# Attention and shared-expert kernel on one core: GpSimd's share of the routing tiles, the order at the pass boundary and at the start, and a matmul on half of the array's rows

## The chip, the cores and the metric

One core of a Trainium2 chip runs the whole program. The metric is the device time of one execution in microseconds. Engines: TensorE (PE; its weight loads are PEld), VectorE (DVE), ScalarE (ACT), GpSimd (POOL) and SyncE (SP), which issues most of the DMAs.

## The reference

64 batches of 128 tokens of 512 numbers, all float32:

```python
x = x + tanh(g_xattn) * attention(layernorm(x), ctx, ctx)    # 32 heads of 16, 8 key/value heads, 128 keys a batch
x = x + tanh(g_ffn) * moe(layernorm(x))

# moe: h is layernorm(x), 8192 tokens
probs = softmax(h @ Wr); topw, topi = top_k(probs, 4); topw /= topw.sum(-1)
shared = silu(h @ Wsg) * (h @ Wsu) @ Wsd * sigmoid(h @ Wse)  # inner width 1408
# the first 64 (token, rank) pairs of each of 32 experts, in token order, go through that expert (inner width 352):
ye = (silu(xe @ Wg) * (xe @ Wu)) @ Wd
out = shared + sum over a token's kept experts of topw * ye
```

## The kernel before

**Attention.** `iterations` runs the batches one after the other on every engine, with the work of several batches interleaved in four steps c = 0 to 3 of a fixed order. PE transposes keys (L645) and queries (L653), computes scores twice: once with queries as rows, for the maxima (L746, into `p_max`), which DVE reduces (L589), and once with keys as rows (L694, into `p_exp`), which ACT exponentiates (L467); then values times probabilities (L669, four tiles of 32 columns), transposes back (L679), transposes the normalised rows (L704) and multiplies with the router's weights (L720). In L694, a step's 128 rows of `kt` hold the stacked parts of two key heads, 64 rows each; the other half of the columns is zero in each, so that one full-height matmul serves one head. ACT's `k_evac` (L444, L445) copies the transposed keys; L669 at c = 0 also waits for it.

At the start DVE clears the padding (`vals`, `qs`, `kt`, `ks`), then takes the statistics of the first batch; POOL computes 1/sqrt (`inverse_root`, L335 and L339), DVE normalises (L537), POOL stacks the high and low parts of keys (`k_stacks`, L347 to L350) and queries (`q_stacks`, L366, L370). POOL's body for batch 0 does them in the order `inverse_root(0)`, `k_stacks(0)`, `q_stacks(0)`, `inverse_root(1)`.

**Shared expert.** The 8192 tokens are 16 tiles of 512. The inner width of 1408 is 11 blocks of 128; the weights of all don't fit on the chip, so there are two passes over the tiles: `Tile(0, i)` with five blocks, `Tile(1, i)` with six. The gate and up products of a block are one 2 x 2 product by Winograd's scheme with seven products (`product`, L1498 to L1500; each in three parts, as every operand is split in a high and a low part). A step f of a tile does: products 1 and 2, then products 6 and 7 of the step before (`last_two`), then 3, 4, 5. DVE adds up (L1427 c11, L1398 c12, L1434 c22), ACT applies SiLU (L1151), DVE multiplies (L1401, L1404), ACT takes the high part `hh` (L1158, `high`), DVE the low part `hl` (L1411, `low`):

```python
                def low(T, f):
                    s = T.step + f
                    dve.wait_ge(hh_done, s + 1)
                    if f == 0:
                        wait(dve, acc_mm, TB * T.n)
                    nc.vector.tensor_tensor(hl[:, f, :], act_g(T), hh[:, f, :].bitcast(F32), ALU.subtract).then_inc(hl_done, 1)
```

`silu` on ACT waits for the low part of the step before, and ACT's copy `term` (L1176) of the next step stands behind it; product 3 waits for `term`, product 7 for c22. At the end of a tile PE does the down products (`down`, L1521 to L1523), four blocks of 128 tokens, and DVE adds each to the output rows (`add_acc`, L1418). Between these adds DVE and ACT prepare the next tile's tokens: loads on SP, four sums (L1249), high parts on ACT (L1144), seven low parts on DVE (L1256).

**Routing.** Tiles 1 to 3 of the first pass carry, in DVE's `work` of each step and one at a tile's end, the search for each expert's first tokens: `key_step` alternates MAX8 (L1307) and MATCH_REPLACE8 (L1309) over 2048 elements; in tile 3 `merge_step` follows. The first step of tile 1 also has `route_weights`. POOL in the meantime splits weights: `down_low` (L1024), `wide_sums` (L1034 to L1040) and the low part of the wide weights for block 5 in one instruction of 1792 elements (L1076). It then waits for the routing.

**Experts.** From tile 4 on, a pair of experts rides on two tiles: `Pair(p, xt, gu, ht, dn)` gives the steps in which PE transposes the gathered rows (L1558), does gate and up (L1567), transposes (L1573) and does down (L1580). In the second of the two tiles `adds` is set: POOL gathers output rows (L1101), DVE adds (`add_rows`, L1344) in steps 1 and 3, POOL scatters them (L1106), first for one expert, then for the other; SP loads the tile's own rows (`load_rows`, L943) when both are through.

**Pass boundary.** The last tile of the first pass, `Tile(0, 15)`, prepares the tokens of tile 0 for `Tile(1, 0)`, as any tile does for its next. In tile 15 POOL runs `wide_sums(1)` to `(5)`, ACT and DVE split the first of these weights (`wide_high(1)`, `wide_low(1)`, L1271), before the first add; the others come in the steps of `Tile(1, 0)`.

The functions that the change touches:

## Time and profile before

| | |
|---|---|
| median of 3 runs | 2221.2 us (2220.02 to 2221.82) |
| the profiled execution | 2219.52 us, its span 2217.7 us |
| granted clock of PE, mean | 0.998 |
| busy: PE, PEld, DVE, ACT, POOL | 98%, 82%, 68%, 53%, 29% |
| the chain that ended last | PE 91%, DVE 5%, issue 1%, DMA 1%, ACT 1% |
| attention | up to about 665 us |
| first pass, second pass | about 665 to 1373 us, 1373 to 2215 us |

A row of the timeline has the start in us, the duration in us (of all that it merges), engine, line, operation, output and inputs, shapes and how many; in brackets the idle time of the engine before it and what ended it. A matmul's record lasts longer than its slot, as matmuls are pipelined: the distance between starts is what it costs. Idle time of an engine that isn't the bottleneck costs nothing.

### The profile page before, as it was taken

The numbers are of one execution on the slowest core, as the hardware profiler recorded it, in microseconds if no ns is written. First come the engines' busy times: TensorE is split into PE (matmuls) and PEld (weight loads), VectorE is DVE, ScalarE is ACT, GpSimd is POOL, SyncE is SP. The second block draws the span as 40 slices with busy tenths as digits, with TensorE's granted clock in tenths as the row PEclk, the third lists the DMA queues.
The fourth block names the chain that finished last, engine by engine and source line by source line (L and its number), as shares of the span: only waits on it lengthen the run. The fifth ranks groups of instructions, "written<-read, shape, count | busy, mean of one in ns | idle before, by whom it ended". The sixth has DMA issues, their size and how long they took to land.

```text
span 2217.7 us, 53973 instructions
## 1 busy us (share of the span) xinstructions
PE 2175.7 (98%) x17121; PEld 1820.9 (82%) x17121; DVE 1517.9 (68%) x3135; ACT 1182.9 (53%) x2365; POOL 652.9 (29%) x1492
## 2 busy tenths in 40 slices
PE   7999999999999999999999999999999999999999
PEld 5777777777768888988888888788898989888888
DVE  6999999999997885655655556655554555555554
ACT  6899999999985333334334434433333333333332
POOL 5778777877773000000100104100010000001100
PEclk9999999999999999999999999999999999999999
DMA  3555555555553324443443444424333423344431
GB/s 87 153 147 152 145 152 146 152 145 152 147 154 124 77 68 157 136 146 116 142 151 102 149 150 148 143 65 147 105 107 100 137 87 127 135 149 153 151 96 62
DMA packets 320316, 286.27 MB, mean 129 GB/s; under 512 B 124753, under 2 KB 238417, under 8 KB 320210
## 3 DMA queue, kind: packets, MB, share of 16 engines
q1 hardware_dynamic: 315858, 272.24, 40.6%
q0 software_dynamic: 4352, 12.65, 2.2%
q8 instruction: 62, 1.02, 0.2%
q14 instruction: 44, 0.36, 0.1%
HBM read 195.43 MB, written 88.34 MB: 128 GB/s over the span
## 4 chain that ended last, share of the span: by engine, by line
PE 91%; DVE 5%; issue 1%; DMA 1%; ACT 1%; POOL 0%; DVEq 0%; ACTq 0%; POOLq 0%; SPq 0%
PE p_a L1498 8%; PE p_a L1499 7%; PE p_a L1500 7%; PE acc L1521 7%; PE acc L1523 6%; PE acc L1522 6%; PE p_pv L669 6%; PE p_max L746 6%; PE p_exp L694 5%; PE p_tq L653 5%; PE p_c L1498 3%; PE p_c L1500 3%; PE p_c L1499 3%; PE p_ot L679 2%; PE p_x L1580 2%; PE p_y L1567 2%
## 5 line engine op out<-in xcount | busy, mean ns | idle before, releaser
L1498 PE MATMUL p_a<-x_h,ws_h 128*128 128x256 f32 x1280 | 374.6, 293 | 11.9 <-DVE chosen L1434 7.4
L1499 PE MATMUL p_a<-x_l,ws_h 128*128 128x256 f32 x1280 | 358.3, 280 | 0.0
L1500 PE MATMUL p_a<-x_h,ws_l 128*128 128x256 f32 x1280 | 357.9, 280 | 0.0
L589 DVE TENSOR_REDUCE negmax<-p_max 128x8 f32<-128x1024 f32 x256 | 313.7, 1225 | 40.9 <-PE p_max L746 38.1
L1151 ACT ACTIVATE chosen<-chosen 128x256 f32<-128x256 f32 x342 | 142.3, 417 | 365.0 <-DVE chosen L1398 208.2
L1521 PE MATMUL acc<-wd_h,hh 128*128 128x512 f32 x704 | 280.1, 398 | 5.1 <-DVE rows L1418 3.7
L1522 PE MATMUL acc<-wd_l,hh 128*128 128x512 f32 x704 | 278.0, 395 | 0.0
L1523 PE MATMUL acc<-wd_h,hl 128*128 128x512 f32 x704 | 278.0, 395 | 0.0
L467 ACT ACTIVATE probs<-p_exp 128x1024 f32<-128x1024 f32 x256 | 261.5, 1021 | 24.0 <-PE p_exp L694 19.6
L1498 PEld LDWEIGHTS p_a<-x_h,ws_h 128*128 128x128 f32 x1280 | 241.1, 188 | 31.9 <-issue 14.4
L1499 PEld LDWEIGHTS p_a<-x_l,ws_h 128*128 128x128 f32 x1280 | 241.9, 189 | 0.6
L1427 DVE TENSOR_TENSOR chosen<-p_b,term 128x256 f32<-128x256 f32 x171 | 72.5, 424 | 246.6 <-PE p_b L1500 152.6
L1500 PEld LDWEIGHTS p_a<-x_h,ws_l 128*128 128x128 f32 x1280 | 241.3, 188 | 0.0
L1084 POOL COPY cur_u<-slot_idx 128x1 uint32 (+1 forms) x16 | 3.7, 230 | 711.1 <-DVE cur_f L1383 594.3
L1144 ACT ACTIVATE x_h<-x_raw 128x512 fp32r<-128x512 f32 x221 | 121.9, 619 | 153.7 <-DVE x_raw L1249 147.7
L1434 DVE TENSOR_TENSOR chosen<-p_a,term 128x256 f32<-128x256 f32 x171 | 72.5, 424 | 175.1 <-PE p_a L1500 174.5
L746 PE MATMUL p_max<-kt,qt 128*128 128x256 f32 x1024 | 184.5, 302 | 1.8 <-DVE negmax L589 1.8
L1498 PE MATMUL p_c<-x_h,ws_h 128*128 128x256 f32 x640 | 180.8, 282 | 0.0
L1499 PE MATMUL p_c<-x_l,ws_h 128*128 128x256 f32 x640 | 179.2, 280 | 0.0
L1176 ACT ACTIVATE term<-p_a 128x256 f32<-128x256 f32 x176 | 66.1, 375 | 212.1 <-PE p_a L1500 207.4
L1500 PE MATMUL p_c<-x_h,ws_l 128*128 128x256 f32 x640 | 179.2, 280 | 0.0
L1521 PEld LDWEIGHTS acc<-wd_h,hh 128*128 128x128 f32 x704 | 132.0, 187 | 46.2 <-issue 9.3
(209 smaller groups left out, 5351.2 us busy)
## 6 DMA issues: line engine op xcount, KB each, us to landing
rows<-out_dram SPq DMA_DIRECT2D x32, 1024.0 KB, 7.2
out_dram<-rows SPq DMA_DIRECT2D x128, 256.0 KB, 2.1
x_raw<-xn_cols SPq DMA_DIRECT2D x124, 256.0 KB, 2.9
ew<-in_L_ffn_Wg_dram SPq DMA_DIRECT2D x32, 704.0 KB, 6.0
ew<-in_L_ffn_Wu_dram SPq DMA_DIRECT2D x32, 704.0 KB, 7.7
xs<-in_x_dram SPq DMA_DIRECT2D x64, 256.0 KB, 2.7
xres<-in_x_dram SPq DMA_DIRECT2D x64, 256.0 KB, 2.8
out_dram<-x SPq DMA_DIRECT2D x64, 256.0 KB, 2.6
```

Source lines behind the costliest of these rows:

```text
L467: nc.scalar.activation(probs[c][:, :], p_exp[:, :, :].rearrange("p a b -> p (a b)"), ACT.Exp, scale=float(D) ** -0.5).then_inc(exp_done, 1)
L589: nc.vector.tensor_reduce(negmax[c // 2][:, :].rearrange("p (g c i) -> p c i g", g=2, c=2)[:, c % 2, :, :], p_max[:, :, :].rearrange("p a ...
L669: last = mm(p_pv[32 * q:32 * q + 32, :], vals[b.par][:, g, :], probs[2 * s + q // 2][:, 512 * (q % 2):512 * (q % 2) + 512], start=True, st ...
L746: last = mm(p_max[:, i // 2, 256 * (i % 2):256 * (i % 2) + 256], qt[B.par][:, c, 128 * i:128 * i + 128], kt[B.par][:, c, :], start=True, s ...
L1144: nc.scalar.activation(x_h[:, k, :, :], block(k), ACT.Copy).then_inc(xhi_done, 1)
L1151: nc.scalar.activation(act_g(T)[:, cols], gate(T)[:, cols], ACT.Silu).then_inc(silu2_done if half else silu1_done, 1)
L1498: mm(bank, w_h[:, a, k, :], x_h[:, b, k, :], start=start and k == 0, stop=False, skip_group_check=not start)
L1499: mm(bank, w_h[:, a, k, :], x_l[:, b, k, :], start=False, stop=False, skip_group_check=not start)
L1500: last = mm(bank, w_l[:, a, k, :], x_h[:, b, k, :], start=False, stop=(k == 1), skip_group_check=not start)
L1521: mm(bank, hh[:, f, t], wd_h[:, d, :], start=(f == 0), stop=False)
L1522: mm(bank, hh[:, f, t], wd_l[:, d, :], start=False, stop=False)
L1523: last = mm(bank, hl[:, f, t], wd_h[:, d, :], start=False, stop=(f == T.nf - 1))
```

## The change

- `qs` and `kt` are cleared by POOL and not by DVE, right after its first constants, counted by a semaphore of their own (`padded`), on which ACT and PE wait; POOL's first batch does `k_stacks(0)` before `inverse_root(0)`.
- L694 for even c: each of the two matmuls reads only its own 64 rows of `kt` and `qt`.
- In tiles 1, 2 and 3 of the first pass the low parts of all steps but the last are taken by POOL (`routed_low`), ahead of its wait for the routing; DVE's `low` does the last one alone and waits for the others.
- POOL's low part of the wide weights is seven instructions, each waited for; `down_low` waits for its own end too.
- The second pass handles the tokens in the order 15, 0, 1, ... 14 (`Tile.data`): `Tile(1, 0)` uses the tokens that `Tile(0, 15)` has on the chip, and neither tile 15 nor the last one prepares tokens (`Tile.loads`); counts of prepared tiles go by `Tile.xn`.
- `wide_low(1)` stands behind the first add of tile 15.
- Pair 0 does its transposes, gate and up, and second transposes one step later, `Pair(p, 1, 2, 3, 4)`; in tile 15 the first `add_rows` comes in step 2 and not 1.

```diff
@@ -202,7 +202,7 @@
             consts, tanh_done = sem("consts"), sem("tanh_done")
-            pads, id0 = sem("pads"), sem("id0")
+            pads, padded, id0 = sem("pads"), sem("padded"), sem("id0")
@@ -325,7 +325,10 @@
                 pool.wait_ge(id0, 3)
-                pool.wait_ge(pads, 8)
+                for i in range(2):
+                    nc.gpsimd.memset(qs[i][:, :, :, :, 0:16], 0.0).then_inc(padded, 1)
+                    nc.gpsimd.memset(kt[i][:, :, :].bitcast(F32), 0.0).then_inc(padded, 1)
+                pool.wait_ge(pads, 5)
@@ -402,8 +405,8 @@
                     if isinstance(B.n, int) and B.n == 0:
+                        k_stacks(B)
                         inverse_root(B, stat1, mv1, ve1, rs1, qraw_done, rs1_done)
-                        k_stacks(B)
@@ -436,7 +439,7 @@
                 nc.scalar.activation(tanh_f[:, :], gf[:, :], ACT.Tanh).then_inc(tanh_done, 1)
-                act.wait_ge(pads, 8)
+                act.wait_ge(padded, 4)
@@ -503,10 +506,6 @@
                     nc.vector.memset(vals[i][:, :, 16:17], 1.0).then_inc(pads, 1)
-                for i in range(2):
-                    nc.vector.memset(qs[i][:, :, :, :, 0:16], 0.0).then_inc(pads, 1)
-                nc.vector.memset(kt[0][:, :, :].bitcast(F32), 0.0)
-                nc.vector.memset(kt[1][:, :, :].bitcast(F32), 0.0).then_inc(pads, 1)
@@ -634,7 +633,8 @@
                 pe.wait_ge(consts, 1)
-                pe.wait_ge(pads, 8)
+                pe.wait_ge(pads, 5)
+                pe.wait_ge(padded, 4)
@@ -691,7 +691,8 @@
                             for g2 in range(2):
-                                last = mm(p_exp[:, g2, :], kt[b.par][:, c, 128 * g2:128 * g2 + 128], qt[b.par][:, c, :],
+                                own = slice(64 * g2, 64 * g2 + 64) if c % 2 == 0 else slice(0, 128)
+                                last = mm(p_exp[:, g2, :], kt[b.par][own, c, 128 * g2:128 * g2 + 128], qt[b.par][own, c, :],
@@ -872,6 +873,23 @@
+                @property
+                def data(self):
+                    if self.part == 0:
+                        return self.i
+                    return NT - 1 if self.at(1, 0) else self.i - 1
+                @property
+                def xn(self):
+                    return self.n - self.part
+                @property
+                def loads(self):
+                    return not (self.last or self.at(0, NT - 1))
@@ -885,7 +903,9 @@
                         t.flip = j * t.nf % 2
-                        pair = Pair(p, 0, 1, 2, 4) if j == 0 and p is not None else None
+                        pair = None
+                        if j == 0 and p is not None:
+                            pair = Pair(p, 1, 2, 3, 4) if isinstance(p, int) and p == 0 else Pair(p, 0, 1, 2, 4)
@@ -973,14 +993,14 @@
                         sp.wait_ge(eo_out, 32 * (adds + 1))
-                    load_rows(T.i)
+                    load_rows(T.data)
...
                         next_down(3)
-                    if not T.last:
-                        i = 0 if T.at(0, NT - 1) else T.i + 1
+                    if T.loads:
+                        i = T.i + 1 - T.part
@@ -999,7 +1019,7 @@
                         sp.wait_ge(add_done, TB * T.n + j + 1)
-                        sp.dma_start(out_rows[bass.ts(TB * T.i + j, 128), :], rows[:, j, :]).then_inc(rows_out, 16)
+                        sp.dma_start(out_rows[bass.ts(TB * T.data + j, 128), :], rows[:, j, :]).then_inc(rows_out, 16)
@@ -1023,6 +1043,7 @@
                                             ALU.subtract).then_inc(dlo_done, 1)
+                    pool.wait_ge(dlo_done, s + 1)
@@ -1073,9 +1094,20 @@
                 pool.wait_ge(wshi_done, 1)
-                nc.gpsimd.tensor_tensor(w5_l[:, :, :, :], raw_slot(0), w5_h[:, :, :, :].bitcast(F32), ALU.subtract).then_inc(wslo_done, 1)
-                pool.wait_ge(route_out, 32)
-                pool.wait_ge(slots_done, 1)
+                for k in range(NW - 1):
+                    chain.inc(nc.gpsimd.tensor_tensor(w5_l[:, k, :, :], raw_slot(0)[:, k, :, :], w5_h[:, k, :, :].bitcast(F32), ALU.subtract))
+                    chain.wait(pool)
+                nc.gpsimd.tensor_tensor(w5_l[:, NW - 1, :, :], raw_slot(0)[:, NW - 1, :, :], w5_h[:, NW - 1, :, :].bitcast(F32),
+                                        ALU.subtract).then_inc(wslo_done, 1)
+                def routed_low(T, f):
+                    s = T.step + f
+                    pool.wait_ge(hh_done, s + 1)
+                    pool.wait_ge(hl_done, s)
+                    if f == 0:
+                        pool.wait_ge(acc_mm, TB * T.n)
+                    nc.gpsimd.tensor_tensor(hl[:, f, :], act_g(T), hh[:, f, :].bitcast(F32), ALU.subtract).then_inc(hl_done, 1)
@@ -1109,6 +1141,11 @@
+                for i in range(1, 4):
+                    for f in range(NF[0] - 1):
+                        routed_low(Tile(0, i), f)
+                pool.wait_ge(route_out, 32)
+                pool.wait_ge(slots_done, 1)
@@ -1223,8 +1260,8 @@
                         wide_high(1)
-                    if not T.last:
-                        split_x(T.n + 1, low_block)
+                    if T.loads:
+                        split_x(T.xn + 1, low_block)
@@ -1345,7 +1382,7 @@
                     wait(dve, add_done, TB * T.n)
-                    nc.vector.tensor_copy(cur_g[:, :], gate_s[:, bass.ts(T.i, TB)]).then_inc(wcur_set, 1)
+                    nc.vector.tensor_copy(cur_g[:, :], gate_s[:, bass.ts(T.data, TB)]).then_inc(wcur_set, 1)
@@ -1383,7 +1420,7 @@
                         scale_rows(e)
-                    if adds is not None and f == 1:
+                    if adds is not None and f == (2 if T.at(0, NT - 1) else 1):
@@ -1405,6 +1442,11 @@
                     s = T.step + f
+                    routed = T.part == 0 and isinstance(T.i, int) and 0 < T.i < 4
+                    if routed and f < T.nf - 1:
+                        return
+                    if routed:
+                        dve.wait_ge(hl_done, s)
@@ -1442,23 +1484,23 @@
                     low(T, T.nf - 1)
-                    if T.at(0, NT - 1):
-                        wide_low(1)
...
                     add_acc(T, 0)
-                    n = T.n + 1
-                    if not T.last:
-                        dve.wait_ge(xb_in, 32 * (T.n + 1))
-                        dve.wait_ge(xa_in, 32 * (T.n + 1))
+                    n = T.xn + 1
+                    if T.at(0, NT - 1):
+                        wide_low(1)
+                    if T.loads:
+                        dve.wait_ge(xb_in, 32 * n)
+                        dve.wait_ge(xa_in, 32 * n)
...
                         route_end()
-                    if not T.last:
+                    if T.loads:
@@ -1493,7 +1535,7 @@
                     if f == 0:
-                        pe.wait_ge(xlo_done, NX * T.n + ORDER.index(b) + 1)
+                        pe.wait_ge(xlo_done, NX * T.xn + ORDER.index(b) + 1)
```

## Rows read from the trace of the kernel before

**Rows 1.** page of the profile, busy time, share and instructions of each engine

```profile
PE 2175.7 (98%) x17121; PEld 1820.9 (82%) x17121; DVE 1517.9 (68%) x3135; ACT 1182.9 (53%) x2365; POOL 652.9 (29%) x1492
```

**Rows 2.** waits of TensorE over the whole span: us in total, times, longest

```profile
PE p_pv L645 <- POOL ks L350: 8.7, 1, 8.7
PE p_a L1498 <- DVE chosen L1434: 7.4, 6, 3.0
PE acc L1521 <- DVE rows L1418: 3.7, 4, 2.9
PE p_x L1558 <- DMA xe<-xn_rows,cur_u: 1.9, 1, 1.9
```

**Rows 3.** windows: 100 to 400 us, busy time (instructions) of each engine, clock, DMA share, GB/s

```profile
100.00:400.00 300.00, 299.95 (x3164) 223.12 (x3163) 284.84 (x628) 273.00 (x462) 236.97 (x611) 1.00 0.56 149
```

**Rows 4.** timeline of the start, GpSimd: start, us, engine, line, operation

```profile
0.74 0.20 POOL L319 MEMSET ident<- 128x128 f32 x1 [0.29 <-POOLq L1643]
6.23 0.24 POOL L335 TENSOR_SCALAR small<-small 128x1 f32<-128x1 f32 x1 [4.42 <-DVE small L528]
8.56 1.51 POOL L366 TENSOR_SCALAR qs<-qraw 128x256 fp32r<-128x256 f32 x4
```

**Rows 5.** timeline, TensorE around its one matmul of 32 rows

```profile
838.44 0.40 PE L1523 MATMUL acc<-wd_h,hl 128*128 128x512 f32 x1
838.76 0.21 PE L1596 MATMUL p_y<-ident,ew 32*64 32x32 f32 x1
838.91 0.50 PE L1521 MATMUL acc<-wd_h,hh 128*128 128x512 f32 x1
```

**Rows 6.** timeline, TensorE around L694 at c = 0 and c = 2

```profile
202.14 0.73 PE L694 MATMUL p_exp<-qt,kt 128*128 128x512 f32 x2
202.80 0.16 PEld L669 LDWEIGHTS p_pv<-probs,vals 128*32 128x32 f32 x8 [0.36 <-ACT kt L445]
207.06 0.62 PE L694 MATMUL p_exp<-qt,kt 128*128 128x512 f32 x2
207.62 1.06 PE L669 MATMUL p_pv<-probs,vals 128*32 128x512 f32 x8
```

**Rows 7.** timeline, the first L1427 of tiles 2 to 6 on VectorE

```profile
763.19 0.41 DVE L1427 TENSOR_TENSOR chosen<-p_b,term 128x256 f32<-128x256 f32 x1
805.58 0.41 DVE L1427 TENSOR_TENSOR chosen<-p_b,term 128x256 f32<-128x256 f32 x1
847.61 0.42 DVE L1427 TENSOR_TENSOR chosen<-p_b,term 128x256 f32<-128x256 f32 x1
898.91 0.42 DVE L1427 TENSOR_TENSOR chosen<-p_b,term 128x256 f32<-128x256 f32 x1 [0.55 <-PE p_b L1500]
937.77 0.42 DVE L1427 TENSOR_TENSOR chosen<-p_b,term 128x256 f32<-128x256 f32 x1 [0.35 <-PE p_b L1500]
```

**Rows 8.** timeline, step 1 of tile 2 on ScalarE and VectorE

```profile
769.06 0.62 ACT L1158 ACTIVATE hh<-chosen 128x512 fp32r<-128x512 f32 x1
771.13 0.68 DVE L1411 TENSOR_TENSOR hl<-chosen,hh 128x512 fp32r<-128x512 f32 x1
772.68 0.42 DVE L1427 TENSOR_TENSOR chosen<-p_b,term 128x256 f32<-128x256 f32 x1 [0.87 <-ACT term L1176]
```

**Rows 9.** timeline, GpSimd and VectorE in step 1 of tile 1

```profile
720.58 1.29 POOL L1024 TENSOR_TENSOR wd_l<-wd_raw,wd_h 128x512 fp32r<-128x512 f32 x1 [20.23 <-ACT wd_h L1130]
721.83 4.05 POOL L1076 TENSOR_TENSOR w_l<-w_raw,w5h_l 128x1792 fp32r<-128x1792 f32 x1
722.38 3.78 DVE L1404 TENSOR_TENSOR chosen<-chosen 128x256 f32<-128x256 f32 x1 [0.15 <-ACT chosen L1151]
```

**Rows 10.** windows: 853.1 to 856.5 us

```profile
853.10:856.50 3.40, 3.40 (x18) 3.40 (x18) 0.85 (x2) 0.80 (x2) 0.00 (x0) 0.50 0.78 294
```

**Rows 11.** timeline, VectorE at the end of tile 15

```profile
1370.04 5.76 DVE L1256 TENSOR_TENSOR x_l<-x_raw,x_h 128x512 fp32r<-128x512 f32 x6
```

**Rows 12.** timeline, GpSimd in tile 15

```profile
1343.53 0.95 POOL L1101 DMA_INDIRECT chosen<-out_dram,cur_u  x1 [2.57 <-DMA out_dram<-chosen,cur_u]
```

## The prediction

> **What bounds the kernel now.** I read the page's engine shares first, then the waits of TensorE, then stretches of the timeline. TensorE (PE) is busy 98% of the span; the next engine, VectorE (DVE), has 68% [rows 1]. So a microsecond counts only where PE loses it: in a wait, in a matmul slot longer than need be, or at half clock. The waits add up to about 40 us, and the large ones have addresses: the first batch's keys (8.7), the second product of the step before, released by DVE's L1434 (7.4), the output adds L1418 (3.7) and the gathered rows of the first expert pair (1.9) [rows 2]. In the attention part nothing shows as a wait (PE 299.95 of 300), but DVE is busy 284.84 of the same 300 us [rows 3]: what PE gives up there, DVE can follow by 5% at most.
>
> **The start.** GpSimd (POOL) sits idle until DVE's first statistics, works `inverse_root` and the key stack from 6.23 and the query stack from 8.56, 2.33 us later [rows 4]. The change puts the clears of `qs` and `kt` on POOL (2 of 512 and 2 of 1024 elements each) and the key stack ahead of `inverse_root`. The nearest POOL row is a clear of 128 elements in 0.20 us [rows 4]; taken to scale beyond a fixed tenth, the four cost about 2.9 us, from 1.9 to 4.9, while the inputs land. Then the same 2.33 of work, now with `inverse_root` last, ends at 7.2. DVE's normalisation (about 0.7) starts no earlier than now, but the query stack follows it at 7.95 and no longer stands behind the key stack until 8.56: **-0.6 us**. The clears could cost nearly nothing (then the same, since the statistics wait for x) or twice as much (+2.9 us on this chain): from -0.6 to +2.3.
>
> **The second score product, L694.** For even c each of its two matmuls now uses 64 rows of the array, one the upper half and one the lower, into two banks. If they run side by side, a slot of 2 x 0.23 becomes one of 0.23. What it costs is a change of the array's shape. The trace has one such change: L1596 (32 rows) starts 0.32 after a 512-column matmul whose slot is 0.23, so 0.09 for draining, and the next full matmul lasts 0.50 where its like last 0.40, because its weights could not be loaded ahead: 0.10 [rows 5]. Today the pair at c = 2 starts at 207.06 and the column-tiled L669 follows at 207.62: 0.56, in which the second change (into L669's shape) is already paid [rows 6]. New: 0.09 + 0.10 + 0.23 + 0.09 = 0.51, a gain of 0.05. At c = 0 the gain would be larger (its slot is 0.66 today), but there L669 is released by the key evacuation on ACT (L445) [rows 6], which hangs on the exponentials and not on this slot; it is clipped to almost nothing. 63 batches x 0.05 is **-3 us**. Bounds: with no price for the change of shape the gain is the whole 0.23 at c = 2, -14.5 us; with no overlap the slots become 0.74 for 0.56 and 0.66, +16 us.
> The Trainium skill (TensorEngine Tiling (Array Packing), Key Properties) says that tiles load weights and multiply independently, and that changing the tiling mode drains the engine. The 0.09 of [rows 5] agrees with the second; no trace here shows two row tiles at once, so the first is what the term rests on beyond the rows. Column tiles do overlap: L669's eight records take 1.06 in all [rows 6].
>
> **Tiles 1 to 3 of the first pass.** They carry the routing steps on DVE. A plain tile takes 937.77 - 898.91 = 38.9 us, tile 2 42.4 and tile 3 42.0 [rows 7]. In their steps DVE runs a key search of 2.3 us, then c22, then the low part L1411 (0.68), and only then may ACT's SiLU, its copy `term` and DVE's next L1427 go: a ring of 5.8 us where PE needs 5.0. In step 1 of tile 2 the high part is there at 769.68, but L1411 comes at 771.13 and ends at 771.81; L1427 follows at 772.68, waiting for ACT's `term` [rows 8]. On POOL the low part starts at once and takes what L1024 takes for the same shape, 1.29 [rows 9]: done at 771.05, 0.76 earlier. The ring falls to about 5.0 and PE bounds it. First steps keep their loss of 0.8 (search before c22, no low part involved), and the merge steps of tile 3 are longer than the searches by half a microsecond. So **-2.4** of tile 2's 3.5 and **-1.4** of tile 3's 3.1.
> Tile 1 is worse: DVE's L1404 lasts 3.78 there and not 0.42, for POOL's L1076 (4.05, one instruction of 1792 elements) holds the memory port [rows 9]. Cut in seven, the product gets in after at most one piece (0.6), and c22 comes 2.8 us earlier. But the same queue now holds the tile's low part: seven pieces at 0.81 (the spacing of POOL's chained 256-element operations) end near 727.8, the low part of step 0 near 729.1, SiLU and `term` at 730.0, against 729.84 to 730.2 now. The wait moves from L1434 to `term`. What is left is the faster ring of the last two steps: **-1.0**. The 2.7 us at 720.6 (route weights and search before c22) stay.
> Does POOL's low part collide with DVE? It runs during the search, which reads one operand; L1404, with two operands in SBUF, is what [rows 9] shows blocked. The Trainium skill (GPSIMD Engine Reference, Key points) speaks against such a move: the two share their SBUF interfaces, with contention for instructions of two SBUF inputs or in a 2-port mode, and elementwise work on VectorE is about twice as fast. 1.29 against 0.68 agrees with the last; whether the search counts as blocked is rival B.
>
> **Tile 4.** `Pair(p, 1, 2, 3, 4)` for pair 0 takes the transposes of the gathered rows one step later. PE now waits 1.9 (2.1 between starts) for them and directly after it the granted clock is 0.50 for 3.4 us, in which 18 matmuls run [rows 10]; at full clock they would have taken about 1.3 less. A step is 5.0 us, so the rows are there: **-3.3**. gate/up to down then has two steps instead of three, as the pairs at the end of the kernel have.
>
> **The pass boundary.** `Tile(1, 0)` takes the tokens of tile 15, so DVE's sums and seven low parts (5.76 for six of them [rows 11]), ACT's copies and four loads on SP fall away, and `wide_low(1)` stands behind the first add. The wait of 2.9 for L1418 [rows 2] and 0.4 of small ones go: **-3.3**. Against it, tile 15's `add_rows(.., 0, y0)` moves from step 1 to step 2, 5.0 us later. POOL begins the scatter about 0.9 after it (1345.0), needs 0.95 for the issue and 2.57 until that has landed, gathers the second half at 1348.5 [rows 12], and this takes the usual 2.9 to land: 1351.4. DVE reaches the second add in step 3 at 1348.4 and stands, with c22, low part and next L1427 queued behind it; PE's second product then waits 0.8 and the one after `term` 0.7: **+1.5**. What follows (the rows of L943, POOL's wide sums) comes 4 us later and has cover, since the x work is gone. The waits of tile (1,0) on `wide_low` and the weight split (3 us) stay. If the second add hid entirely, this part is -3.3; if also the rows came late, about 0.
>
> The waits between `down_low`s cost POOL 0.1 each, hidden in tile 0.
>
> **Sum.** -0.6 - 3.0 - 1.0 - 2.4 - 1.4 - 3.3 - 3.3 + 1.5 = -13.5. The profiled execution took 2219.5 (span 2217.7): 2206.0. The median of the runs is 1.7 above it: **2207.7 us**.
>
> **Rivals.**
> A, slower: the two half-height matmuls do not overlap, and both changes of shape are paid on top. +16 in place of -3: 2226.7. For it: no row tiles in this trace. Against: the column tiles. It decides as soon as a batch loses 0.17 us, which is its whole overlap at c = 2.
> B: DVE's search and POOL's low part exclude each other. The low part then ends after the search as now, or 0.6 later: the 4.8 of tiles 1 to 3 are gone, at worst 3 more: 2212.5 to 2215.5. For it: [rows 9]. Against: in attention POOL is busy 237 of 300 us and DVE still fills 285, most of it with one operand from SBUF or PSUM [rows 3].
> C: the change of shape is hidden as the loads are ahead of it: 2207.7 - 11.5 = 2196.
> D: the two weight loads follow one another (0.10): +0.05 a batch instead of -0.05: 2214.
>
> **Chances.** The forecast's case (2201 to 2212) 0.62; C 0.09; D 0.10; B 0.08; A 0.07; mixtures around 2218 0.04. Range 2197 to 2216. 0.2% (4.4 us) is about what a measurement of this kernel can tell from no change; below 2216.8 lies 0.88, between 0.05, above 2225.6 0.07.
>
> **What would show it.** Right: in attention the two L694 of even c start within 0.02 us and the batch takes 10.0 us; L1427 in tile 2 every 5.0; no wait at L1558, no clock drop in tile 4; no wait for L1418 at tile 15 but one in its step 3 or 4. Wrong: a batch longer than 10.05; L1307 stretched beyond 2.3 beside POOL's low part; POOL clears over 3 us at the start.

## The result, and the profile after

The changed kernel takes 2207.6 us (median of 4 runs, 2207.3 to 2208.7) against 2220.8 (4 runs, 2220.0 to 2221.8): ratio 0.9942, 95% interval 0.9930 to 0.9953. The forecast was 2207.7. The total came out; of its terms three were well off, and they partly cancelled. Executions of one kernel also differ among themselves by more than some of the terms: the profiled one of before lies 1.3 us under its median, that of after (2208.68, span 2206.9) 1.1 over, so that the spans differ by 10.8 us and the medians by 13.2. A stage below is read from one execution of each kernel.

The page of the kernel after, its first line of busy times (as in [rows 1]), and TensorE's longest waits (as in [rows 2]; L1540, L1563, L1476 and L1460 are the old L1498, L1521, L1434 and L1418):

```profile
PE 2171.8 (98%) x17121; PEld 1817.3 (82%) x17121; DVE 1493.6 (68%) x3108; ACT 1177.5 (53%) x2358; POOL 668.1 (30%) x1514
```

```profile
PE p_a L1540 <- DVE chosen L1476: 6.0, 6, 2.5
PE p_pv L645 <- POOL ks L353: 6.0, 1, 6.0
PE p_tq L653 <- POOL qs L373: 3.7, 1, 3.7
PE p_a L1540 <- ACT term L1213: 2.8, 4, 1.8
...
PE acc L1563 <- DVE rows L1460: 0.5, 2, 0.3
```

PE is as busy as before by share. The wait for the gathered rows (1.9) is gone; what waited for L1418 (3.7) has shrunk to 0.5. The wait for L1476 went from 7.4 to 6.0 only, and the wait for the query stack has grown from 1.8 to 3.7. The time by stages, from the starts of the second score product and the end of DVE's fourth output add of each tile in both traces (us; tile 16 is `Tile(1, 0)`):

| stage | forecast | before | after | change |
|---|---|---|---|---|
| start, to the first second score product | -0.6 | 22.05 | 22.65 | +0.6 |
| first to last of these products | -3.0 | 639.93 | 636.97 | -3.0 |
| from there to the end of tile 0 | 0 | 53.88 | 53.85 | 0.0 |
| tile 1 | -1.0 | 47.41 | 46.75 | -0.7 |
| tile 2 | -2.4 | 42.39 | 40.01 | -2.4 |
| tile 3 | -1.4 | 41.82 | 39.33 | -2.5 |
| tile 4 | -3.3 | 50.89 | 47.16 | -3.7 |
| tiles 5 to 14 | 0 | 433.87 | 433.92 | +0.1 |
| tiles 15 and 16 (pass boundary) | -1.8 | 103.38 | 104.12 | +0.7 |
| rest of the span | 0 | 782.09 | 782.14 | +0.1 |
| sum | -13.5 | 2217.7 | 2206.9 | -10.8 |

**Attention.** The timeline of the kernel after at a c = 2, as in [rows 6] (start, us, engine, line, operation):

```profile
206.02 0.71 PE L747 MATMUL p_max<-kt,qt 128*128 128x256 f32 x4
206.66 0.50 PE L695 MATMUL p_exp<-qt,kt 64*128 64x512 f32 x2
207.09 1.06 PE L669 MATMUL p_pv<-probs,vals 128*32 128x512 f32 x8
```

The pair is now one group of 0.50, its two records 0.003 apart, and the column-tiled product follows 0.43 after its start. From the start of the last first-score matmul to the product with the values that makes 0.64, where it was 0.67 (medians of the slots at c = 2). The gain at c = 2 is thus 0.034 us, or 2.1 us over 63 batches; the rest of the 3.0 comes from elsewhere in the batch. At c = 0 the product with the values is still held by the keys' evacuation, but stands 0.05 us behind it in half the batches, where it stood 0.14: the slot there is 0.03 to 0.09 shorter. The stretch itself differs between executions: with row halves at even c alone (the kernel after and ten of the experiments) it took 636.4 to 638.4 us, at full height (before, experiment 1) 639.9 and 640.2. The slots, not the single difference, are what the term rests on. The 100 to 400 us window, against [rows 3]:

```profile
100.00:400.00 300.00, 299.98 (x3178) 221.65 (x3176) 286.69 (x630) 272.74 (x464) 237.82 (x616) 1.00 0.56 150
```

DVE has gone from 284.84 to 286.69 of 300: it follows.

**Tile 2.** GpSimd's low parts and the searches on VectorE in steps 0 to 2:

```profile
766.75 1.28 POOL L1110 TENSOR_TENSOR hl<-chosen,hh 128x512 fp32r<-128x512 f32 x1 [23.73 <-ACT hh L1195]
771.70 1.30 POOL L1110 TENSOR_TENSOR hl<-chosen,hh 128x512 fp32r<-128x512 f32 x1 [3.67 <-ACT hh L1195]
```

```profile
770.14 0.42 DVE L1441 TENSOR_TENSOR chosen<-chosen 128x256 f32<-128x256 f32 x1 [0.15 <-ACT chosen L1188]
...
770.55 2.28 DVE L1346 MATCH_REPLACE8 ew<-ew 128x2048 f32<-128x2048 f32 x1
...
773.87 0.43 DVE L1469 TENSOR_TENSOR chosen<-p_b,term 128x256 f32<-128x256 f32 x1 [0.58 <-ACT term L1213]
```

The low part starts at once and ends at 773.00, beside a search of 2.28 that it does not stretch. L1469 comes every 4.97 us (768.90, 773.87), where it came every 5.8.

### The profile page after: what moved, and what is told of

Read it like the earlier page. It is cut to its first block, busy times and chain, and to the rows that moved or that the text cites. A ratio compares the mean times of both kernels' runs of the same rounds, so it can differ in the third digit from the quotient of the medians.

```text
span 2206.9 us, 53964 instructions
## 1 busy us (share of the span) xinstructions
PE 2171.8 (98%) x17121; PEld 1817.3 (82%) x17121; DVE 1493.6 (68%) x3108; ACT 1177.5 (53%) x2358; POOL 668.1 (30%) x1514
## 3 DMA queue, kind: packets, MB, share of 16 engines
q8 instruction: 62, 1.02, 0.2%
## 4 chain that ended last, share of the span: by engine, by line
PE 92%; DVE 3%; issue 2%; POOL 1%; DMA 1%; ACT 0%; DVEq 0%; SPq 0%; POOLq 0%; ACTq 0%
PE p_a L1540 8%; PE p_a L1541 7%; PE acc L1563 7%; PE p_a L1542 7%; PE acc L1565 7%; PE acc L1564 7%; PE p_pv L669 6%; PE p_max L747 6%; PE p_tq L653 5%; PE p_exp L695 5%; PE p_c L1540 3%; PE p_c L1542 3%; PE p_c L1541 3%; PE p_ot L679 2%; PE p_x L1622 2%
## 5 line engine op out<-in xcount | busy, mean ns | idle before, releaser
L1540 PE MATMUL p_a<-x_h,ws_h 128*128 128x256 f32 x1280 | 374.5, 293 | 9.9 <-DVE chosen L1476 6.0
L1563 PE MATMUL acc<-wd_h,hh 128*128 128x512 f32 x704 | 279.8, 397 | 2.8 <-DVE hl L1453 1.3
L1540 PEld LDWEIGHTS p_a<-x_h,ws_h 128*128 128x128 f32 x1280 | 241.8, 189 | 28.6 <-issue 14.4
L1469 DVE TENSOR_TENSOR chosen<-p_b,term 128x256 f32<-128x256 f32 x171 | 72.6, 425 | 247.1 <-PE p_b L1542 151.8
L1476 DVE TENSOR_TENSOR chosen<-p_a,term 128x256 f32<-128x256 f32 x171 | 72.5, 424 | 177.4 <-PE p_a L1542 176.7
L1540 PE MATMUL p_c<-x_h,ws_h 128*128 128x256 f32 x640 | 180.1, 281 | 0.0
L1563 PEld LDWEIGHTS acc<-wd_h,hh 128*128 128x128 f32 x704 | 132.0, 187 | 42.8 <-issue 9.8
```

What stands on the lines that cost most here:

```text
L1540: mm(bank, w_h[:, a, k, :], x_h[:, b, k, :], start=start and k == 0, stop=False, skip_group_check=not start)
L1563: mm(bank, hh[:, f, t], wd_h[:, d, :], start=(f == 0), stop=False)
```

## The experiments

All times are medians. Experiments 1 to 4, 5 to 8 and 9 to 12 ran on one chip each, the kernel before beside them at 2220.3, 2219.9 and 2220.6; across these groups, and against the kernel after (its before: 2220.8), differences under 1 us mean little.

### 1. Full height for every c

```diff
-own = slice(64 * g2, 64 * g2 + 64) if c % 2 == 0 else slice(0, 128)
+own = slice(0, 128)
```

> The changed kernel with the second score product at full height for every c. If the row halves are what shortens the batch (my theory), the span from the first to the last of these products grows back from 637.0 us to about 640.0, and the pair at c = 2 takes 0.67 from the start of the matmul before it to the first product with the values, instead of 0.64; the two matmuls start 0.23 apart and not 0.003. In all +3 us. The rival, that GpSimd's or VectorE's smaller work at the start has shifted the pipeline, leaves the batch at 10.02 us.

Measured: 2208.8 us. Attention, first to last second score product, 640.19 against 636.97: +3.2, as expected. At c = 2:

```profile
207.74 0.72 PE L747 MATMUL p_max<-kt,qt 128*128 128x256 f32 x4
208.30 0.62 PE L695 MATMUL p_exp<-qt,kt 128*128 128x512 f32 x2
208.85 0.64 PE L669 MATMUL p_pv<-probs,vals 128*32 128x512 f32 x4
```

0.56 + 0.55 between the same three starts, against 0.64 + 0.43: the full-height pair begins 0.08 earlier behind its neighbour and needs 0.12 longer. The median rose by 1.2 only (1.7, if each is taken against its own runs of the kernel before): the term is read from the stage and the slots, since the start and tile 15 differ between executions by as much (below).

### 2. Row halves for odd c too

```diff
-own = slice(64 * g2, 64 * g2 + 64) if c % 2 == 0 else slice(0, 128)
+own = slice(64 * g2, 64 * g2 + 64)
```

> The changed kernel with row halves for odd c too, where the neighbours on both sides are full-height matmuls. The change of shape is then paid on both sides (drain and a weight load that isn't ahead, 0.09 + 0.10, then again): 0.21 + 0.42 = 0.63 from the start of the matmul before to the start of the matmul behind, against 0.585 now, so 126 x 0.05 = +6 us if TensorE bounds the odd slots. The rival, that the way back into a full-height matmul costs only the drain, gives 0.21 + 0.33 = 0.54 and -5 us.

Measured: 2217.3 us, attention 646.67, that is +9.7. An odd slot of this kernel:

```profile
206.53 0.72 PE L747 MATMUL p_max<-kt,qt 128*128 128x256 f32 x4
207.18 0.50 PE L695 MATMUL p_exp<-qt,kt 64*128 64x512 f32 x2
207.62 0.55 PE L705 MATMUL p_pv<-ident,xn 128*128 128x128 f32 x3
```

From the start of the last first-score matmul to that of the product behind the pair it is 0.636 in the median of 109 slots, where full height takes 0.585. So a row-tiled pair costs 0.64 whatever stands behind it, and pays only where the full-height slot is over that: beside a column-tiled neighbour (0.67), whose change of shape is paid in any case. 126 x 0.05 explains 6.4 of the 9.7; the batch grows to 10.17 us, and where the other 3 go was not tried.

### 3. The first add of tile 15 at step 1

```diff
-if adds is not None and f == (2 if T.at(0, NT - 1) else 1):
+if adds is not None and f == 1:
```

> The changed kernel with the first add of the expert rows in the last tile of the first pass back at step 1. In the changed kernel TensorE waits 1.95 + 0.57 there and then runs at half clock from 1343.5 to 1346.2. If the late first add is the cause, the second half's rows are there at the second add, both waits and the half clock go, and tiles 14 to 16 take 3.5 to 4 us less (from 104.1 to about 100.5). Rival: the first half's rows land just behind step 1, so VectorE stands there instead; then the wait moves one step and the gain is under 2 us.

Measured: 2204.0 us; tile 15 takes 38.95 instead of 43.00, tile 16 the same 61.1: -4.0. First the kernel after in tile 15, GpSimd's scatter of the first half and gather of the second, and VectorE's two adds (L1381), then this one's adds:

```profile
1333.42 0.93 POOL L1138 DMA_INDIRECT out_dram<-chosen,cur_u  x1 [8.59 <-DVE chosen L1381]
1337.29 0.96 POOL L1133 DMA_INDIRECT chosen<-out_dram,cur_u  x1 [2.94 <-DMA out_dram<-chosen,cur_u]
```

```profile
1331.83 0.68 DVE L1381 TENSOR_TENSOR chosen<-top,chosen 64x512 f32<-64x512 f32 x1
...
1341.06 0.68 DVE L1381 TENSOR_TENSOR chosen<-ebuf,chosen 64x512 f32<-64x512 f32 x1 [4.16 <-DMA chosen<-out_dram,cur_u]
```

```profile
1326.41 0.68 DVE L1381 TENSOR_TENSOR chosen<-top,chosen 64x512 f32<-64x512 f32 x1
...
1336.30 0.68 DVE L1381 TENSOR_TENSOR chosen<-ebuf,chosen 64x512 f32<-64x512 f32 x1
```

In the kernel after, the first add at 1331.83 lets the scatter go at 1333.42, the gather at 1337.29 lands 3.7 later, and DVE stands 4.16 us before the second add, with the next L1476 queued behind it. With the add a step earlier nothing is waited for. Behind the stall TensorE's clock fell to 0.50 in the kernel after. Experiment 4 has the same stall, 2.85 us later, and its clock stayed at 1.00 (the window holds the stall and what follows):

```profile
1343.50:1346.20 2.70, 2.69 (x12) 2.69 (x13) 1.59 (x5) 0.80 (x2) 0.81 (x2) 0.50 0.22 49
```

```profile
1342.00:1350.00 8.00, 6.01 (x43) 5.30 (x42) 4.26 (x10) 2.29 (x6) 2.46 (x4) 1.00 0.25 57
```

With a stretch at 0.50 tile 15 takes 43.0 and 43.2 (the kernel after, experiment 2), without one 41.7 to 42.0 (experiments 1, 4, 5, 6). The stall isn't quite the same in the six: TensorE waited 2.5 and 2.6 us in the two whose clock fell, and 2.0 to 2.3 in the other four, as scatter and gather together took 6.7 and 6.8 us to land in the former and 6.2 to 6.5 in the latter. So of the 1.0 to 1.5 us between the two groups 0.2 to 0.6 are the longer wait and 0.8 to 1.0 the clock. The forecast counted on a landing of 2.9 us. That was the usual gather; in tile 15 of the kernel before the two gathers had taken 3.0 and 3.7, the second being the one that now stands in the way (the two of L1101 there, from issue to landing):

```profile
DMA to landing us min/median/max: 3.0/3.4/3.7
```

### 4. Low parts on VectorE again

```diff
-for i in range(1, 4):
-    for f in range(NF[0] - 1):
-        routed_low(Tile(0, i), f)
...
-routed = T.part == 0 and isinstance(T.i, int) and 0 < T.i < 4
+routed = False
```

> The changed kernel with the low parts of tiles 1 to 3 back on VectorE; the weight split stays in seven pieces. If the move to GpSimd made the ring of the routing steps shorter (my theory), tiles 2 and 3 take 42.4 and 41.8 again, +2.4 and +2.5. Tile 1: the pieces alone should give it about 1 us less than with the low part on GpSimd behind them, or the same. In all +4 to +5 us. Rival: the pieces, not the place of the low part, gave tile 1's gain, and tile 1 stays at 46.7 or goes under.

Measured: 2210.6 us, 3.0 above the kernel after (3.5 against each one's own runs of the kernel before) and not 4 to 5: tiles 2 and 3 take 42.40 and 41.82, the times of before, but tile 1 takes 44.92, 1.8 and not 1 less than with the move (46.75). The rival holds for tile 1, the theory for tiles 2 and 3. GpSimd and VectorE of the kernel after in step 1 of tile 1, then VectorE of this one:

```profile
719.55 5.00 POOL L1098 TENSOR_TENSOR w_l<-w_raw,w5h_l 128x256 fp32r<-128x256 f32 x6
724.63 0.74 POOL L1100 TENSOR_TENSOR w_l<-w_raw,w5h_l 128x256 fp32r<-128x256 f32 x1
725.33 1.26 POOL L1110 TENSOR_TENSOR hl<-chosen,hh 128x512 fp32r<-128x512 f32 x1
```

```profile
720.27 0.41 DVE L1441 TENSOR_TENSOR chosen<-chosen 128x256 f32<-128x256 f32 x1
...
722.96 0.42 DVE L1476 TENSOR_TENSOR chosen<-p_a,term 128x256 f32<-128x256 f32 x1
727.46 0.42 DVE L1469 TENSOR_TENSOR chosen<-p_b,term 128x256 f32<-128x256 f32 x1 [4.07 <-ACT term L1213]
```

```profile
719.90 0.59 DVE L1438 TENSOR_TENSOR chosen<-chosen 128x256 f32<-128x256 f32 x1 [0.15 <-ACT chosen L1185]
...
723.07 1.02 DVE L1450 TENSOR_TENSOR hl<-chosen,hh 128x512 fp32r<-128x512 f32 x1
724.96 0.42 DVE L1466 TENSOR_TENSOR chosen<-p_b,term 128x256 f32<-128x256 f32 x1 [0.87 <-ACT term L1210]
```

The seven pieces take 5.8 us, the low part stands behind them until 726.6, and L1469 waits 4.07 for `term`. On VectorE the low part starts at 723.07 and ends at 724.1, although it takes 1.02 beside the pieces and not 0.68. Tile 1 itself differs between executions of the order with GpSimd's low part there: 46.3 in experiments 1, 5 and 6, where PE's clock fell to 0.50 once in it, 46.6 to 46.8 in the kernel after and experiments 2 and 3, where it fell twice.

### 5. The first pair at steps 0, 1, 2, 4

```diff
-pair = Pair(p, 1, 2, 3, 4) if isinstance(p, int) and p == 0 else Pair(p, 0, 1, 2, 4)
+pair = Pair(p, 0, 1, 2, 4)
```

> The changed kernel with the first expert pair at steps 0, 1, 2 and 4 again. My theory: TensorE then waits about 2 us for the gathered rows at the first step and runs some 3 us at half clock behind it; tile 4 goes from 47.2 to 50.9 us, +3.7 in all. Rival: the gather now comes a few us after the routing as before, but tiles 1 to 3 are shorter, so that the rows are later still for TensorE: over +5.

Measured: 2206.1 us, no worse than the kernel after. Tile 4 takes 48.23, +1.1 and not +3.7: TensorE waits 0.83 for the rows, and the clock does not fall behind it (wait, then window):

```profile
841.14 0.66 PE L1600 MATMUL p_x<-ident,xe 128*128 128x128 f32 x4 [0.83 <-DMA xe<-xn_rows,cur_u]
```

```profile
841.00:844.50 3.50, 3.36 (x29) 3.36 (x30) 0.85 (x2) 1.08 (x3) 0.00 (x0) 1.00 1.07 379
```

So 1.1 of the 3.7 us come back here. The rest is not shown to belong to anything in the change. The gather starts as long before TensorE's need of it as in the kernel before (5.6 us); what differs is its landing, 6.4 us after its issue here and 7.5 in the kernel before, and this same gather lands after 6.2 to 6.8 us in eleven of the fourteen profiled executions and after 7.1 to 7.5 in three (the kernel before, experiments 2 and 3). In an execution with a late landing the early steps would wait some 1.9 again, by this account, and the moved steps save more; the medians (2206.1 here, 2207.6 for the kernel after, on different chips) don't settle it. With the shorter wait the half clock was absent too. Neither theory had that; nothing bears out the rival's "later still".

### 6. inverse_root first again

```diff
-k_stacks(B)
 inverse_root(B, stat1, mv1, ve1, rs1, qraw_done, rs1_done)
+k_stacks(B)
 q_stacks(B)
```

> The changed kernel with inverse_root ahead of the first key stack again; the clears stay on GpSimd. In the changed kernel the first transposes start at 5.96 but the next only at 10.75, and TensorE's matmuls take half-clock times until 22 to 25 us, where those of the kernel before go to full speed at 17. Theory: with the keys 1.2 us later and the queries some 0.4 earlier the gap shrinks from 3.7 to about 2.2 us, the matmuls are fast from about 17 us, and the first second score product starts at 21.2 instead of 22.65: -1 us. Rival: where the clock rises has nothing to do with this gap (it differs from execution to execution of one kernel); then it stays at 22 to 25 and the start gains 0.4 at most.

Measured: 2206.6 us. The first query columns come at 10.24 instead of 10.75, but the first second score product at 22.62: the matmuls were slow until 27.7 us in the profiled execution. In this execution the shorter gap did not bring the clock up sooner, and the time of the start turns out to go by when the clock rises. Three executions, TensorE: the kernel before, the kernel after, and experiment 5, which has the start of the kernel after:

```profile
14.24 1.20 PE L746 MATMUL p_max<-kt,qt 128*128 128x256 f32 x4
...
16.85 0.71 PE L746 MATMUL p_max<-kt,qt 128*128 128x256 f32 x4 [0.40 <-DVE negmax L589]
...
22.05 0.63 PE L694 MATMUL p_exp<-qt,kt 128*128 128x512 f32 x2
```

```profile
10.75 1.12 PE L653 MATMUL p_tq<-ident,qs 128*128 128x128 f32 x4 [3.70 <-POOL qs L373]
...
15.99 1.20 PE L747 MATMUL p_max<-kt,qt 128*128 128x256 f32 x4 [0.40 <-DVE negmax L588]
...
22.01 0.71 PE L747 MATMUL p_max<-kt,qt 128*128 128x256 f32 x4
22.65 0.49 PE L695 MATMUL p_exp<-qt,kt 64*128 64x512 f32 x2
```

```profile
16.00 0.71 PE L747 MATMUL p_max<-kt,qt 128*128 128x256 f32 x4 [0.40 <-DVE negmax L588]
...
21.29 0.50 PE L695 MATMUL p_exp<-qt,kt 64*128 64x512 f32 x2
```

The same four first-score matmuls take 1.20 or 0.71 as a group. With the clock up by 16.0 the first second score product comes at 21.3 (experiments 5 and 7), by 22 at 22.7 (the kernel after, 2, 3), from 24 on at 23.0 to 23.2 (1, 4, 12; in 9, where it rose at 27.8, at 23.1 too). So against 22.05 the new order gains 0.75 (forecast 0.6) in executions in which the clock rises at 16; in others it loses up to 1.1. One profiled execution of each kernel can't tell a change of the start from this scatter, experiment 6 included. The column of the granted clock says 1.00 for all of it (kernel after, 12 to 16 us). That is no reading: the traces have no record of the clock ahead of the rise (the first begins at 16.83 in the kernel before, 21.95 in that after, 15.65 in experiment 5, 27.43 in 6), and the column counts what has no record as 1.00. There the durations have to be read:

```profile
12.00:16.00 4.00, 2.96 (x13) 2.42 (x13) 1.38 (x2) 1.47 (x3) 0.89 (x3) 1.00 0.00 0
```

### 7. First add at step 1, low parts of tiles 2 and 3 only

```diff
-for i in range(1, 4):
+for i in range(2, 4):
     for f in range(NF[0] - 1):
         routed_low(Tile(0, i), f)
...
-routed = T.part == 0 and isinstance(T.i, int) and 0 < T.i < 4
+routed = T.part == 0 and isinstance(T.i, int) and 1 < T.i < 4
```

> The changed kernel with the first add of the last tile at step 1, and GpSimd's low parts in tiles 2 and 3 alone. With the low parts on VectorE tile 1 took 44.92 and not 46.75; so this should take 2204.0 - 1.8 = 2202.2 us, with tiles 1, 2 and 3 at 44.9, 40.0 and 39.3. Rival: with GpSimd's queue empty in tile 1 its share of tile 2 changes something too (the weight split's last pieces beside VectorE), and the gain is smaller.

Measured: 2202.2 us; tiles 1 to 3 take 44.91, 40.00 and 39.36, as expected.

### 8. TensorE kept at work at the start

```diff
+for _ in range(20):
+    tr(p_ot[:, 0:128], ident[:, :], ident[:, :])
...
 k_cols(B)
+for _ in range(24):
+    tr(p_ot[:, 0:128], ident[:, :], ident[:, :])
 q_cols(B, 0)
```

> The kernel above (first add at step 1, low parts of tiles 2 and 3) with 20 transposes of the identity on TensorE ahead of the first key columns and 24 behind them, into a bank that nobody reads then; so that it has work from 1.6 us on. If its clock rises by the work it does (theory), the matmuls have full-clock times by 10.8 us, the second score product begins at 19.5 to 20.5 instead of 22 to 23, and the time falls by 2 to 3 us. Rival: the clock rises at a time of its own, and the time stays, or grows by the transposes that run into the first query columns.

Measured: 2200.3 us, 1.9 less and not 2 to 3. The transposes go from a slot of 0.213 to 0.109 at 4.8 us, but the matmuls from 12.2 to 15.2 and again from 18.5 are slow, and here the granted clock says so:

```profile
12.00:15.00 3.00, 2.80 (x12) 2.39 (x12) 0.82 (x1) 0.66 (x2) 0.90 (x3) 0.50 0.00 0
```

The first second score product starts at 21.44 and not by 20.5. The clock's record rises at 4.8 with the transposes, falls to 0.50 at 11.7, behind a gap of 1.55 us (before 10.77), and again at 18.5, behind one of 1.32 (before 17.58). Whether the gaps let it fall is what experiment 10 tries.

### 9. The weight split in one piece (on 7)

```diff
-for k in range(NW - 1):
-    chain.inc(nc.gpsimd.tensor_tensor(w5_l[:, k, :, :], ...))
-    chain.wait(pool)
-nc.gpsimd.tensor_tensor(w5_l[:, NW - 1, :, :], ...).then_inc(wslo_done, 1)
+nc.gpsimd.tensor_tensor(w5_l[:, :, :, :], ...).then_inc(wslo_done, 1)
```

> The kernel with the first add at step 1 and the low parts of tiles 2 and 3 on GpSimd, but the weight split of tile 1 in one instruction again. If the seven pieces are what shortens tile 1 (theory), VectorE's product in step 1 lasts 3.8 us again and tile 1 takes 47.4 us instead of 44.9. Rival: with the search of tile 1 where it is now the product does not meet the split, and tile 1 stays at 45.

Measured, a single run: 2207.4 us, 4.7 above experiment 12, the same kernel but for this on the same chip. Tile 1 takes 47.87 and not 44.90, which is 3.0 of it; 1.0 stands in attention, which the edit doesn't touch. VectorE's product in step 1 is blocked as in [rows 9]:

```profile
721.83 3.88 DVE L1437 TENSOR_TENSOR chosen<-chosen 128x256 f32<-128x256 f32 x1
```

### 10 to 12. The gaps filled

The transposes `fill(n)` are those of 8. Experiment 12 is 7 once more. Experiment 10 is 8 with 38 in place of 24 transposes, and

```diff
 q_cols(B, 0)
+fill(9)
...
+if c == 2 and isinstance(B.n, int) and B.n == 0:
+    fill(10)
...
+if c == 1 and isinstance(B.n, int) and B.n == 0:
+    fill(6)
```

Experiment 11 is 10 with the order of 6, and with 30 transposes ahead of the key columns and 18 behind them in place of 20 and 38.

> The kernel with the first add at step 1 and the low parts of tiles 2 and 3 on GpSimd, once more, to stand beside the next two on one chip. 2202 us; the first second score product at 21.3 if the clock is up by 16 us, at 22.7 to 23.0 if it is not.

> The same with transposes of the identity in every gap of TensorE in the first batch: 20 ahead of the key columns, 38 behind them, 9 behind the first query columns, 6 and 10 in the waits for VectorE's maxima. With the first 44 alone the matmuls were at full-clock times from 4.8 us, but at half-clock times again at 12.2 and 18.5. Theory: with the gaps filled they stay at full-clock times, the first second score product starts at 20.0, and the time is 2 to 2.5 us under the kernel without the transposes. Rival: the clock falls back at 12 us whatever the work, and the time is that of the 44 transposes (1.9 under) or worse by transposes that delay query columns.

> The same with inverse_root ahead of the first key stack (30 transposes ahead of the key columns, 18 behind them). The first query columns come at 10.24 instead of 10.76, so 0.5 us less if nothing else in the first batch is later. Rival: the keys' evacuation, 1.4 us later, is then what the first maxima wait for, and nothing is gained.

Measured: 2202.7, 2200.2 and 2199.0 us, the last 0.9903 of the kernel before (0.9888 to 0.9918), the fastest here. TensorE in 10:

```profile
10.77 0.66 PE L659 MATMUL p_tq<-ident,qs 128*128 128x128 f32 x4
...
12.61 0.72 PE L758 MATMUL p_max<-kt,qt 128*128 128x256 f32 x4
...
20.01 0.49 PE L703 MATMUL p_exp<-qt,kt 64*128 64x512 f32 x2
```

All matmuls have full-clock times from 6 us on, and the first second score product starts at 20.01 (in 11 at 19.37, in 12 at 23.16). So with the gaps filled the clock did not fall back at 12, and the rival of 10 falls; 11 gained 1.2 where 0.5 was expected, 0.64 of it ahead of that product. The runs of 10 lie within 0.2 us, those of 11 within 0.25; the five of 12 spread over 2.3. Experiments 7 and 12 are one kernel: its clock rose at 15.8 and 24.2, the product came at 21.30 and 23.16, and the spans were 2199.0 and 2200.9, so the whole difference of 1.9 was made at the start. Most of the scatter of this kernel seems to be that.

## Why the prediction was right, and where it was not

**Row-tiled L694, right in kind (-3.0 for -3.0).** The pair with both changes of shape takes 0.52 (forecast 0.51, before 0.55; I had taken 0.56 from one place). That is 0.034 a batch or 2.1 us, not 0.05; c = 0, which I had clipped to nothing, gave a little too, and the batch fell by 0.05. To hit 3.0 was in part luck. Experiment 1 gives it back. Rivals A, C and D fall: the two matmuls run side by side; getting in costs 0.09 over the usual slot of 0.12, and the way out 0.20 over the 0.23 of one matmul, against 0.09 before. By the Trainium skill (TensorEngine Tiling (Array Packing), Key Properties) tiles work independently and a change of mode drains; the 0.003 between the records and the 0.05 that experiment 2 loses at each odd c agree.

**Tiles 2 and 3, right, tile 3 mis-sized.** Experiment 4 gives both back. Tile 2 is the forecast's. In tile 3 I let the merge steps keep 1.7 of the loss; the ring there was bound by the same low part, and 2.5 of the 3.1 went. Rival B falls: a search of 2.28 beside a low part of 1.30 stays 2.28. What collides with GpSimd's instruction is VectorE's product of two operands in SBUF (3.88 in experiment 9). The Trainium skill (GPSIMD Engine Reference, Key points) names just these instructions, and those in a 2-port mode; the trace agrees for the first.

**Tile 1: the sum (-0.7 for -1.0; -0.7 to -1.2 over six executions) was right, the judgement behind it incomplete.** The wait did move from L1434 to `term`, which comes at 727.5, in the time of before 729.9; forecast 730.0. Experiments 4, 7, 9 and 12 show that the pieces alone are worth 2.5 to 3.0 us and that the low part on GpSimd takes 1.3 to 1.8 of it back.

**Tile 4, -3.7 for -3.3, the cause shown for 1.1 of it.** The step "the rows are there: -3.3" gave the whole wait and the half clock to `Pair(p, 1, 2, 3, 4)`. With the reorder no execution waits there. Experiment 5 gives back 1.1; in it the other 2.6 were absent without the reorder. There the rows landed 1.1 sooner after their issue than in the one profiled execution of before, which is the shorter wait, and the clock stayed up. As the landing scatters by as much between executions, how much of the 2.6 is chance stays open.

**Pass boundary: the reuse right, the add mis-sized.** Without the later add, tiles 15 and 16 take 38.95 + 61.12 = 100.07, 3.3 less than before, as forecast. The term "+1.5" for the add measured +4.0, or +2.7 to +3.0 where the clock held. I took the gather's landing as the usual 2.9 after its issue; it was 3.7, as it had been for this gather in the kernel before, and GpSimd waited 2.9 for the scatter instead of 2.57. DVE therefore stood 4.2 us and not 3.0; PE waited 1.95 + 0.57 and not 0.8 + 0.7. And I left the half clock behind such a wait out, though [rows 10] showed it.

**Start, mis-sized with the wrong sign in this profile (+0.6 for -0.6).** The chain of instructions was read rightly (query columns 0.86 earlier, the four clears 2.8 us, from 1.86 to 4.63). What the sum did not hold is that the matmuls of the first batch run at half-clock times until a moment that differs between executions; in experiments 5 and 7, where they are fast by 16, the same start comes to -0.75.

The misses were +1.2 (start), +2.5 (add) and +0.3 (tile 1) against -1.1 (tile 3) and -0.4 (tile 4); with 0.2 in the stages without a term that is 2.7, the -13.5 of the forecast against -10.8. The medians differ by 13.2 because the execution profiled of the kernel before lies under its median and that of after above; a start and a tile 15 with the clock up are worth 1.4 and 1.0 to 1.3, but in which runs they fell isn't on record. That the forecast of 2207.7 met 2207.6 was luck: the misses cancelled in part, and the scatter covered the rest.

## What to carry to other kernels

A step moved by one position in a hand-made order moves every transfer chained behind it: add up issue, landing and the return trip from the rows of these very transfers or the longest, not the usual ones, and compare with where the next user stands; here one step cost 4 us in tile 15 (3.6 by the medians), beside the 13 gained in all. Cut a long GpSimd instruction that runs beside VectorE's two-operand work, and put nothing urgent behind the pieces. Filling TensorE's gaps in the first batch with transposes that nobody reads bought 2.5 us here, and the runs then lay within 0.25 us.

## What the hardware did that I had not expected

Kernels with the same start reached full speed at 16, 22, 24 or 28 us in different executions, one and the same kernel at 15.8 and 24.2 (experiments 7 and 12), while the granted clock in the windows read 1.00 for want of a record; only the durations (415 against 280 ns for a 256-column matmul) tell. With TensorE at work from 1.5 us on (experiments 8, 10 and 11) it was up by 6 us, and in 8 it fell again to 0.50 behind gaps of 1.55 and 1.32 us. In tile 15 waits of 2.5 and 2.6 us were followed by half clock, and waits of 2.0 to 2.3 us in four other executions were not; in tile 4 a wait of 1.9 was and one of 0.8 was not. But the length of the wait doesn't decide alone: TensorE's first wait in tile 1 is 2.5 us in all fourteen profiled executions, and half clock followed within 1.5 us in eight of them and not in six. The gather of the first pair's rows lands 6.2 to 7.5 us after its issue, depending on the execution.
